# Reordering the softmax step of a fused attention and expert kernel: maxima first, the spread of the inverse sums between the exponentials

## The chip, the cores and the metric

One core of one Trainium2 chip runs the whole program. The metric is the time of one execution on the device in microseconds (us), as the median of several executions. The profiler records one execution; its span runs from its first to its last instruction.

## What is computed

The reference is one layer of cross attention and one feed-forward layer with a shared expert and eight routed experts, for 32 batches of 112 tokens with 512 channels, all in float32:

```python
x = x + attention(layernorm(x), ctx)      # 16 heads of 32 channels, causal
x = x + ffn(layernorm(x))                 # top 2 of 8 experts (352 wide) + a shared one (1408 wide)

# attention
scores = einsum('bhqd,bhkd->bhqk', qh, kh) / sqrt(32)
attn = softmax(where(causal, scores, min))
out = einsum('bhqk,bhkd->bhqd', attn, vh) @ Wout.T
```

The causal mask leaves only the first 112 of the 375 context rows for 112 queries, so the kernel works on 112 by 112 scores for each of the 16 heads of a batch. The softmax is computed as exp(score − maximum) without its division; the product with the values is divided by the row's sum afterwards.

## The kernel before

The program has three stages, one after the other: the attention with the norms and the router (stage A), the routed experts in 35 jobs of 256 tokens, and the shared expert with the final sum. The change touches stage A alone.

Stage A works on groups of four batches (g = 0 to 7, then two more rounds to drain what is under way). A group has a front and four steps (j = 0 to 3). The front transposes the normalised rows of the four batches, splits them into a high and a low part (`xT_hi` L811 on ScalarE, `xT_lo` L1133 on VectorE) and makes kT and qT, with 48 matmuls for qT alone. A step t = 4g + j works on several batches at once: the scores and exponentials of batch t, the transposed exponentials, value product and division of batch t−1, the output projection of batch t−2, and the second norm, its transposition and the router of batch t−3. A product of split operands is made of three matmuls on high and low parts, in the helper `product` (L542), so one line holds the q, k, value, projection and expert matmuls alike; they are told apart by their tiles.

The order of work on each engine is the order of the code; engines wait for each other by semaphores. There is no planner: the order is written by hand, separately in the program of each engine. In one step it is:

- TensorE: mask (L587) and scores (L596) into PSUM banks 0 to 3; transposes of the exponentials (`probsT`, L605); their products with the values of the batch (`outT`, L616); transposes of the spread inverse sums (`sumT`, L624), behind a wait for `rinv_spread`; the value product (into bank 4); the transposes of `xn2` (`normT`, L637); the projection (12 matmuls, `wout`, also into bank 4); the router (L660). At j = 2 of groups from 2 on, the rank matmuls (L667, L668) follow.
- ScalarE: four copies of `probsT` (L834); `rinv_wide` (L839), which spreads the 16 inverse sums of a row over 32 channels each; 8 exponentials (L849, each an ACTIVATE with an accumulator read); `rinvT` (L827), the copy of the transposed inverse sums; 8 exponentials; `aT_hi` (L860). At j = 3 two small exponentials of the router (L820, L821) come first.
- VectorE: `rinv` (L1142); the statistics of an input batch for the next group (L1093, L1096); `xn2` (L1099); at j = 0 the first choice of experts of the group before (`choose`, L1259 to L1274, ten chained small operations), at j = 3 the slots (`place`, L1294 to L1296, six operations); the maxima in two halves (`smax` L1159, `minus_max` L1161); `v_sb` (L1166), which empties bank 4; `xn2T` (L1174); `attnT` (L1181), the division; at j = 1 the second choice (L1277 to L1285); `xn` of the next group (L1099); `x` (L1196), which adds the projection; `logits` (L1201); at j = 2 the rank (L1207); statistics of `x1`; `aT_lo` (L1216). After step 2 the router's maxima (L1241 to L1243) follow.
- GpSimd: the inverse roots of the norms (L975, L977), at j = 3 the split of the next context (L984, L986), and eight indirect DMAs of token numbers (L1010) per group. The DMA queue of SP stores x1, the normalised rows and their transposes, and loads the next inputs.

The projection of a step takes bank 4 behind `v_sb`, which has to have emptied the value product from it:

```python
b = take(g, j, "proj")     # waits until bank 4 has been emptied as often as it was taken
product(bank(b, SEQ), [((aT_hi[...], aT_lo[...]), (wout_hi[...], wout_lo[...])) for k in range(KC)])
```

`TURNS` (L48 to L56) lists, for each bank from 4 to 7, which stage uses it after which; the counts of all `filled` and `emptied` waits come from it.

Of the kernel before, what the change touches and what calls it, by code (L numbers as in the profile page):

```python
# [14 lines left out]
P = 128  # L15
SEQ = 112
# [34 lines left out]
for _j in range(TB):  # L51
    TURNS += [((_j, "probsT", k), 1, (7, 5, 4, 6)[k]) for k in range(4)]
    TURNS += [((_j, "outT", 0), 1, 7), ((_j, "sumT", 0), 1, 5), ((_j, "value", 0), 0, 4),
              ((_j, "normT", 0), 3, 6), ((_j, "proj", 0), 2, 4), ((_j, "router", 0), 3, 6)]
    if _j == 2:
        TURNS += [((_j, "rank", 0), 2 * TB, 4)]  # L56
# [33 lines left out]
def build_program(nc, x, ctxT, wq, wkv, wout, gates, w_experts, w_shared, out):  # L90
# [17 lines left out]
    with ctx:  # L108
# [427 lines left out]
        def _(pe):  # L536
# [39 lines left out]
            def step(g, j):  # L576
# [42 lines left out]
                if there(g, j, 1):  # L619

                    pe.wait_ge(S["rinv_spread"], t)
                    b = take(g, j, "sumT")
                    for m in range(KC):
                        mm = pe.transpose(psum[:, b, m * SEQ:(m + 1) * SEQ], rinv_wide[:, 4 * m:4 * m + 4, :].rearrange("s h d -> s (h d)"),  # L624
                                          ident[0:SEQ, 0:SEQ])
                    mm.then_inc(filled[b], 1)
# [12 lines left out]

                def proj():  # L640
                    if there(g, j, 2):

                        if is_first(g):
                            pe.wait_ge(S["w_split"], 3)
                        pe.wait_ge(S["attnT_split"], t - 1)
                        b = take(g, j, "proj")
                        product(bank(b, SEQ), [((aT_hi[:, j % 2, k, :], aT_lo[:, j % 2, k, :]), (wout_hi[:, k, :], wout_lo[:, k, :]))
                                               for k in range(KC)]).then_inc(filled[b], 1)


                for part in ((proj, normT) if isinstance(g, int) and g >= NG else (normT, proj)):
                    part()
# [137 lines left out]
        def _(act):  # L790
# [7 lines left out]
            def body(g):  # L798
# [17 lines left out]
                for j in range(TB):  # L816
                    t = g * TB + j
                    if j == TB - 1 and there(g, 0, 4):
                        act.wait_ge(S["router_z"], 2 * g)
                        act.activation(rt["e"][:, :, :], rt["z"][:, :, :], ACT.Exp).then_inc(S["router_exp"], 1)  # L820
                        act.activation(rt1["ge"][:, :], rt1["g"][:, :], ACT.Exp, scale=-1.0).then_inc(S["router_exp"], 1)  # L821
                    def rinv_to_rows():
                        b = turns.bank("sumT")
                        if there(g, j, 2):
                            wait_emptied(act, g, j - 1, "outT")
                        wait_filled(act, g, j, "sumT")
                        act.activation(rinvT[:, :], bank(b, P, GT), ACT.Copy).then_inc(emptied[b], 1)  # L827

                    if there(g, j, 1):
# [6 lines left out]
                        if there(g, j, 2):  # L836
                            wait_filled(act, g, j - 1, "sumT")
                        act.wait_ge(S["rinv_made"], t)
                        act.activation(rinv_wide[:, :, :], rinv[:, :].unsqueeze(2).to_broadcast([SEQ, HEADS, HD]), ACT.Copy).then_inc(S["rinv_spread"], 1)  # L839
                        if not there(g, j, 0):  # L840
                            rinv_to_rows()
                    if there(g, j, 0):

                        at_least(act, S["rinv_made"], t - 1)
                        for i in range(2):
# [7 lines left out]
                            if i == 0 and there(g, j, 1):  # L853
                                rinv_to_rows()
                    if there(g, j, 1):

                        if there(g, j, 3):
                            wait_filled(act, g, j - 1, "proj")
# [220 lines left out]
        def _(dve):  # L1079
# [55 lines left out]
            def step(g, j):  # L1135
                t = g * TB + j
                if there(g, j, 1):
# [4 lines left out]
                    dve.reciprocal(rinv[:, :], rsum[:, (j + 1) % 2, :]).then_inc(S["rinv_made"], 1)  # L1142
                if before(g, NG - 1):
                    stats1(j, t + TB + 1, g + 2)
# [9 lines left out]
                if there(g, j, 0):  # L1154

                    dve.wait_ge(S["scores_done"], t + 1)
                    for i in range(2):
                        scores = psum[0:SEQ, 2 * i:2 * i + 2, 0:GT].rearrange("s r (m k) -> s r m k", m=4)
                        dve.tensor_reduce(smax[:, 2 * i:2 * i + 2, :], scores, AX.X, ALU.max).then_inc(S["smax_made"], 1)  # L1159
                        dve.wait_ge(S["smax_made"], 2 * t + i + 1)  # L1160
                        dve.tensor_scalar(minus_max[:, 2 * i:2 * i + 2, :], smax[:, 2 * i:2 * i + 2, :], -SCALE, None, ALU.mult).then_inc(S["max_made"], 1)  # L1161
                if there(g, j, 0):

# [11 lines left out]
                if there(g, j, 1):  # L1175

                    at_least(dve, S["attnT_split"], t - 1)
                    b = turns.bank("outT")
                    wait_emptied(dve, g, j, "sumT")
                    wait_filled(dve, g, j, "outT")  # L1180
                    dve.tensor_tensor(attnT[:, :], bank(b, P, GT), rinvT[:, :], ALU.mult).then_inc(emptied[b], 1)  # L1181
# [15 lines left out]
                if there(g, j, 3):  # L1197
# [3 lines left out]
                    dve.tensor_copy(logits[:, (j + 1) % TB, :], bank(b, SEQ, EXPERTS + 1)).then_inc(emptied[b], 1)  # L1201
                if j == 2 and routes(g):
# [294 lines left out]
```

## Time and profile before

| | |
|---|---|
| median of 3 executions | 1716.71 us (1716.38 to 1719.96) |
| profiled execution | 1713.32 us, span 1711.5 us |
| TensorE matmul busy | 1586.7 us (93% of the span) |
| VectorE busy | 883.5 us (52%) |
| ScalarE busy | 616.5 us (36%) |
| GpSimd busy | 463.2 us (27%) |
| mean granted TensorE clock | 0.972 of full speed |

The shares are means over the three stages. Stage A takes about the first 530 us; in it VectorE and ScalarE are busy half of the time or more, while they are mostly idle in the other two stages. Times in the trace are counted from the start of the span. A matmul's duration is modelled and overlaps the next one's, so the starts of matmuls tell more than their durations; the same holds for VectorE and ScalarE, where an instruction's record overlaps the next by about 0.1 us.

### The profile page before, as it was taken

What the parts mean: (1) busy time and instruction counts of PE and PEld (TensorE: products, weight loads), DVE (VectorE), ACT (ScalarE), POOL (GpSimd) and SP (SyncE); (2) the same over time, 40 slices, a digit from 0 to 9 for tenths busy, and PEclk for the clock granted to TensorE, in tenths of its full rate; (3) what the DMA queues carried; (4) which work ended last, traced back from release to release, by engine and by line L of the source; (5) the groups of instructions that cost most, each with busy time, mean ns of one, the idle gap of its engine ahead of it and who ended that gap; (6) DMA issues with size and microseconds to landing.
All of it is one profiled execution on the core that took longest, in us unless ns stands there. A gap on an engine that the chain in (4) does not pass through costs nothing.

```text
span 1711.5 us, 30372 instructions
## 1 busy us (share of the span) xinstructions
PE 1586.7 (93%) x10524; PEld 1329.2 (78%) x10524; DVE 883.5 (52%) x1724; ACT 616.5 (36%) x1945; POOL 463.2 (27%) x424
## 2 busy tenths in 40 slices
PE   4899899889993599999999999999999999999998
PEld 4677767767772499999999997888888888888886
DVE  4556675676565467676667675442232323232322
ACT  4766676576670232333332333321111111111111
POOL 3111312313213455655555550201000000000010
PEclk9899999999995699999999999999999999999999
DMA  5122322322122466666666664413020203021110
GB/s 186 52 61 86 87 83 59 86 80 75 43 87 44 152 236 238 259 243 240 240 232 249 244 254 161 140 70 111 13 99 25 98 25 98 25 86 36 50 49 25
DMA packets 82445, 202.43 MB, mean 118 GB/s; under 512 B 37424, under 2 KB 38448, under 8 KB 77648
## 3 DMA queue, kind: packets, MB, share of 16 engines
q1 hardware_dynamic: 70208, 168.44, 28.6%
q0 software_dynamic: 12176, 33.20, 5.9%
q8 instruction: 35, 0.57, 0.1%
q14 instruction: 26, 0.21, 0.1%
HBM read 153.64 MB, written 47.97 MB: 118 GB/s over the span
## 4 chain that ended last, share of the span: by engine, by line
PE 79%; DVE 8%; ACT 5%; issue 3%; DMA 1%; POOL 1%; another core or an unknown queue 1%; DVEq 0%; SPq 0%; ACTq 0%; POOLq 0%
PE psum L542 51%; PE psum L776 12%; PE psum L726 9%; ACT probs L849 2%; PE psum L699 2%; ACT probsT L834 2%; DVE smax L1159 2%; DVE stat L1093 1%; PE psum L596 1%; DVE v_sb L1166 1%; PE psum L587 1%; PE psum L605 1%; POOL lists_dram L1010 1%; PE psum L660 1%
## 5 line engine op out<-in xcount | busy, mean ns | idle before, releaser
L542 PE MATMUL psum<-nT_hi,ws_hi 128*128 128x512 f32 x616 | 243.1, 395 | 3.5 <-DVE nT_lo L1374 3.5
L542 PE MATMUL psum<-nT_hi,ws_lo 128*128 128x512 f32 x616 | 244.9, 398 | 0.0
L542 PE MATMUL psum<-nT_lo,ws_hi 128*128 128x512 f32 x616 | 244.4, 397 | 0.0
L1413 DVE TENSOR_TENSOR h_s<-psum,silu_s 128x512 f32<-128x512 f32 x77 | 53.2, 692 | 364.8 <-PE psum L542 360.5
L542 PE MATMUL psum<-gT_hi,wj_hi 128*128 128x256 f32 (+1 forms) x840 | 233.9, 278 | 1.2 <-DVE gT_lo L1345 1.2
L542 PE MATMUL psum<-gT_lo,wj_hi 128*128 128x256 f32 (+1 forms) x840 | 233.4, 278 | 0.0
L542 PE MATMUL psum<-gT_hi,wj_lo 128*128 128x256 f32 (+1 forms) x840 | 233.3, 278 | 0.0
L1072 POOL DMA_INDIRECT routed<-expert_out_dram,slot_b x56 | 55.2, 986 | 575.4 <-DVE slot_b L1426 383.2
L849 ACT ACTIVATE probs<-psum,minus_max 112x112 f32<-112x112 f32 x512 | 175.2, 412 | 16.5 <-DVE minus_max L1161 16.4
L1034 POOL TENSOR_SCALAR wj_hi<-wj_raw 128x2816 fp32r<-128x2816 f32 x68 | 136.8, 2028 | 145.1 <-PE psum L726 118.4
L1364 DVE TENSOR_TENSOR wj_lo<-wj_raw,wj_hi 128x2816 fp32r<-128x2816 f32 x70 | 170.3, 2434 | 5.7 <-issue 3.3
L542 PEld LDWEIGHTS psum<-gT_hi,wj_hi 128*128 128x128 f32 (+1 forms) x840 | 151.3, 180 | 8.0 <-issue 4.0
L542 PEld LDWEIGHTS psum<-gT_lo,wj_hi 128*128 128x128 f32 (+1 forms) x840 | 151.4, 180 | 2.4
L542 PEld LDWEIGHTS psum<-gT_hi,wj_lo 128*128 128x128 f32 (+1 forms) x840 | 151.4, 180 | 0.0
L939 ACT ACTIVATE silu_s<-psum 128x512 f32<-128x512 f32 x77 | 46.0, 598 | 286.4 <-PE psum L542 286.4
L1045 POOL DMA_INDIRECT xg<-normed_dram,job_ids x70 | 131.7, 1881 | 58.6 <-DMA job_ids<-lists_dram 44.6
L542 PEld LDWEIGHTS psum<-nT_hi,ws_hi 128*128 128x128 f32 x616 | 116.2, 189 | 31.9 <-issue 4.0
L542 PEld LDWEIGHTS psum<-nT_lo,ws_hi 128*128 128x128 f32 x616 | 115.9, 188 | 28.2
L542 PEld LDWEIGHTS psum<-nT_hi,ws_lo 128*128 128x128 f32 x616 | 116.1, 188 | 27.4
L849 ACT ACTIVATION_READ_ACCUMULATOR probs<-psum,minus_max 112x1 f32 x512 | 136.0, 266 | 0.0
L942 ACT ACTIVATE hs_hi<-h_s 128x512 fp32r<-128x512 f32 x77 | 48.7, 632 | 233.5 <-DVE h_s L1413 227.5
L776 PE MATMUL psum<-ws_lo,hs_hi 128*128 128x512 f32 x308 | 121.4, 394 | 0.0
(193 smaller groups left out, 3108.4 us busy)
## 6 DMA issues: line engine op xcount, KB each, us to landing
wj_raw<-in_w_experts SPq DMA_DIRECT2D x35, 2176.0 KB, 8.6
expert_out_dram<-y_c SPq DMA_DIRECT2D x35, 512.0 KB, 2.7
wj_raw<-in_w_shared SPq DMA_DIRECT2D x11, 768.0 KB, 4.4
x_in<-in_x SPq DMA_DIRECT2D x32, 224.0 KB, 3.5
x_res<-in_x SPq DMA_DIRECT2D x32, 224.0 KB, 3.0
x_dram<-x SPq DMA_DIRECT2D x32, 224.0 KB, 2.3
normed_dram<-xn SPq DMA_DIRECT2D x32, 224.0 KB, 3.1
normedT_dram<-xn2T SPq DMA_DIRECT2D x32, 224.0 KB, 3.5
```

What stands on the lines that cost most here:

```text
L542: mm = pe.matmul(out_ap, u, v, start=(n == 0), stop=(n == last))
L699: mm = pe.transpose(psum[:, b, j * P:(j + 1) * P], xg[p][:, j, k * P:(k + 1) * P], ident[:, :])
L726: mm = pe.matmul(bank(j), u, v, start=(i == 0 and q == 0), stop=(i == 2 and q == 2))
L776: mm = pe.matmul(bank(j), u, v, start=(i == 0 and q == 0), stop=(i == SC - 1 and q == 2))
L849: done = act.activation(probs[:, j % 2, 4 * r + m, :], psum[0:SEQ, r, m * SEQ:(m + 1) * SEQ], ACT.Exp, bias=minus_max[:, r, m:m + 1], scal ...
L939: act.activation(silu_s[:, :], bank(b), ACT.Silu).then_inc(emptied_b[b], 1)
L942: act.activation(hs_hi[:, i % 2, :], h_s[:, :], ACT.Copy).then_inc(S["hs_hi_made"], 1)
L1034: pool.tensor_scalar(wj_hi[p][:, part], wj_raws[p][:, part], 1.0, 0.0, ALU.mult, ALU.add).then_inc(S["wc_hi_made"], 1)
L1045: pool.indirect_dma_start(out=xg[p][:, j, :], out_offset=None, in_=normed_dram, in_offset=bass.IndirectOffsetOnAxis(ap=job_ids[p][:, j:j + ...
L1072: pool.indirect_dma_start(out=routed[:, b % 2, c, :], out_offset=None, in_=expert_out_dram, in_offset=bass.IndirectOffsetOnAxis(ap=slot_b[ ...
L1364: dve.tensor_tensor(wj_lo[p][:, cols], wj_raws[p][:, cols], wj_hi[p][:, cols].bitcast(F32), ALU.subtract).then_inc(S["wc_split"], 1)
L1413: dve.tensor_tensor(h_s[:, :], bank(b), silu_s[:, :], ALU.mult).then_inc(emptied_b[b], 1)
```

## The change

Three engines' programs are reordered; no operation is added or taken away.

1. VectorE: the maxima and their negated, scaled copies stand right behind `rinv`, ahead of the statistics, `xn2`, `choose` and `place`.
2. ScalarE: `rinv_wide` moves from ahead of the exponentials to between their two halves (where `rinvT` was), and `rinvT` moves behind the second half, ahead of `aT_hi`. Where a step has no exponentials (the drain), `rinv_wide` follows the `probsT` copies directly.
3. TensorE: the `sumT` transposes move from ahead of the value product to behind the `normT` transposes and ahead of the projection (in the drain: ahead of both). `TURNS` is reordered to match.
4. VectorE: `attnT`, which needs `rinvT`, moves from ahead of `xn` to behind `logits`.

```diff
--- before.py
+++ after.py
     TURNS += [((_j, "probsT", k), 1, (7, 5, 4, 6)[k]) for k in range(4)]
-    TURNS += [((_j, "outT", 0), 1, 7), ((_j, "sumT", 0), 1, 5), ((_j, "value", 0), 0, 4),
-              ((_j, "normT", 0), 3, 6), ((_j, "proj", 0), 2, 4), ((_j, "router", 0), 3, 6)]
+    TURNS += [((_j, "outT", 0), 1, 7), ((_j, "value", 0), 0, 4),
+              ((_j, "normT", 0), 3, 6), ((_j, "sumT", 0), 1, 5), ((_j, "proj", 0), 2, 4), ((_j, "router", 0), 3, 6)]
@@ TensorE
-                if there(g, j, 1):
-
-                    pe.wait_ge(S["rinv_spread"], t)
-                    b = take(g, j, "sumT")
-                    for m in range(KC):
-                        mm = pe.transpose(psum[:, b, m * SEQ:(m + 1) * SEQ], rinv_wide[:, 4 * m:4 * m + 4, :].rearrange("s h d -> s (h d)"),
-                                          ident[0:SEQ, 0:SEQ])
-                    mm.then_inc(filled[b], 1)
...
+                def sums():
+                    if there(g, j, 1):
+
+                        pe.wait_ge(S["rinv_spread"], t)
+                        b = take(g, j, "sumT")
+                        for m in range(KC):
+                            mm = pe.transpose(psum[:, b, m * SEQ:(m + 1) * SEQ], rinv_wide[:, 4 * m:4 * m + 4, :].rearrange("s h d -> s (h d)"),
+                                              ident[0:SEQ, 0:SEQ])
                         mm.then_inc(filled[b], 1)
...
-                for part in ((proj, normT) if isinstance(g, int) and g >= NG else (normT, proj)):
+                for part in ((sums, proj, normT) if isinstance(g, int) and g >= NG else (normT, sums, proj)):
                     part()
@@ ScalarE
+                    def rinv_across():
+                        if there(g, j, 2):
+                            wait_filled(act, g, j - 1, "sumT")
+                        act.wait_ge(S["rinv_made"], t)
+                        act.activation(rinv_wide[:, :, :], rinv[:, :].unsqueeze(2).to_broadcast([SEQ, HEADS, HD]), ACT.Copy).then_inc(S["rinv_spread"], 1)
+
...
-                        if there(g, j, 2):
-                            wait_filled(act, g, j - 1, "sumT")
-                        act.wait_ge(S["rinv_made"], t)
-                        act.activation(rinv_wide[:, :, :], rinv[:, :].unsqueeze(2).to_broadcast([SEQ, HEADS, HD]), ACT.Copy).then_inc(S["rinv_spread"], 1)
                         if not there(g, j, 0):
-                            rinv_to_rows()
+                            rinv_across()
...
                             if i == 0 and there(g, j, 1):
-                                rinv_to_rows()
+                                rinv_across()
                     if there(g, j, 1):
 
+                        rinv_to_rows()
                         if there(g, j, 3):
                             wait_filled(act, g, j - 1, "proj")
                         wait_emptied(act, g, j, "outT")
@@ VectorE
                     dve.reciprocal(rinv[:, :], rsum[:, (j + 1) % 2, :]).then_inc(S["rinv_made"], 1)
+                if there(g, j, 0):
+
+                    dve.wait_ge(S["scores_done"], t + 1)
+                    for i in range(2):
+                        ...
                 if before(g, NG - 1):
                     stats1(j, t + TB + 1, g + 2)
...
-                if there(g, j, 0):
-
-                    dve.wait_ge(S["scores_done"], t + 1)
-                    for i in range(2):
-                        ...
...
-                if there(g, j, 1):
-
-                    at_least(dve, S["attnT_split"], t - 1)
-                    b = turns.bank("outT")
-                    wait_emptied(dve, g, j, "sumT")
-                    wait_filled(dve, g, j, "outT")
-                    dve.tensor_tensor(attnT[:, :], bank(b, P, GT), rinvT[:, :], ALU.mult).then_inc(emptied[b], 1)
...
                     dve.tensor_copy(logits[:, (j + 1) % TB, :], bank(b, SEQ, EXPERTS + 1)).then_inc(emptied[b], 1)
+                if there(g, j, 1):
+
+                    at_least(dve, S["attnT_split"], t - 1)
+                    b = turns.bank("outT")
+                    wait_emptied(dve, g, j, "sumT")
+                    wait_filled(dve, g, j, "outT")
+                    dve.tensor_tensor(attnT[:, :], bank(b, P, GT), rinvT[:, :], ALU.mult).then_inc(emptied[b], 1)
```

## Rows read from the trace of the kernel before

**Rows 1.** Waits in 40 to 505 us: engine, line, releaser, us in total, times, longest.

```profile
PE psum L542 <- DVE v_sb L1166: 26.7, 30, 2.4
...
ACT probs L849 <- DVE minus_max L1161: 13.8, 12, 1.6
```

**Rows 2.** Timeline of step j = 1, group 4: start us, us, engine, line, instruction.

```profile
284.60 0.48 PE L542 MATMUL psum<-wout_hi,aT_hi 128*112 128x512 f32 x1 [0.40 <-DVE v_sb L1166]
...
287.67 0.69 DVE L1196 TENSOR_TENSOR x<-psum,x_res 112x512 f32<-112x512 f32 x1 [0.98 <-PE psum L542]
...
290.15 1.75 PE L605 MATMUL psum<-ident,probs 112*112 112x112 f32 x16
...
290.78 1.84 ACT L834 ACTIVATE probsT<-psum 112x448 f32<-112x448 f32 x4 [2.05 <-PE psum L605]
...
292.49 0.65 ACT L839 ACTIVATE rinv_wide<-rinv 112x512 f32<-112x512 f32 x1
...
293.01 0.38 ACT L849 ACTIVATE probs<-psum,minus_max 112x112 f32<-112x112 f32 x1
...
293.20 0.61 PE L624 MATMUL psum<-ident,rinv_wide 112*128 112x112 f32 x4
...
293.57 0.47 PE L542 MATMUL psum<-wkv_hi,ctx_hi 128*112 128x512 f32 x1
...
294.55 0.69 DVE L1166 COPY v_sb<-psum 112x512 f32<-112x512 f32 x1 [0.57 <-PE psum L542]
...
295.30 0.48 PE L542 MATMUL psum<-wout_hi,aT_hi 128*112 128x512 f32 x1 [0.40 <-DVE v_sb L1166]
...
295.64 0.62 ACT L827 ACTIVATE rinvT<-psum 128x448 f32<-128x448 f32 x1
...
296.29 0.62 DVE L1181 TENSOR_TENSOR attnT<-psum,rinvT 128x448 f32<-128x448 f32 x1 [0.52 <-ACT rinvT L827]
```

**Rows 3.** Timeline of step j = 2, group 4, the same columns.

```profile
302.12 0.64 DVE L1093 BATCH_NORM_STATS2 stat<-x_in 112x6 f32<-112x512 f32 x1
...
303.47 1.08 DVE L1159 TENSOR_REDUCE smax<-psum 112x8 f32<-112x896 f32 x1
...
305.89 0.69 DVE L1166 COPY v_sb<-psum 112x512 f32<-112x512 f32 x1
...
306.63 0.49 PE L542 MATMUL psum<-wout_hi,aT_hi 128*112 128x512 f32 x1 [1.06 <-DVE v_sb L1166]
```

**Rows 4.** Timeline of step j = 3, group 4, and the start of the next front.

```profile
311.17 0.19 DVE L1207 TENSOR_TENSOR rt_rank<-psum,list_at 112x32 f32<-112x32 f32 x1 [0.59 <-PE psum L668]
...
318.12 1.13 POOL L986 TENSOR_TENSOR ctx_lo<-ctx_in,ctx_hi 128x448 fp32r<-128x448 f32 x1
318.40 0.88 DVE L1161 TENSOR_SCALAR minus_max<-smax 112x8 f32<-112x8 f32 x1
...
319.92 0.48 PE L542 MATMUL psum<-wout_hi,aT_hi 128*112 128x512 f32 x1 [2.35 <-DVE v_sb L1166]
...
323.11 0.68 ACT L860 ACTIVATE aT_hi<-attnT 128x448 fp32r<-128x448 f32 x1
...
324.13 0.98 ACT L811 ACTIVATE xT_hi<-psum 128x448 fp32r<-128x448 f32 x2 [0.35 <-PE psum L559]
```

**Rows 5.** Timeline of front and step j = 0, group 4 (267 to 284 us), and the next projection.

```profile
270.34 0.19 DVE L1259 TENSOR_REDUCE rt_s<-rt_e 112x4 f32<-112x32 f32 x1 [1.23 <-DMA route_dram<-route]
...
272.48 0.19 DVE L1274 TENSOR_TENSOR rt_one<-prefer,route 112x32 f32<-112x32 f32 x1
...
279.68 1.09 DVE L1159 TENSOR_REDUCE smax<-psum 112x8 f32<-112x896 f32 x1 [7.00 <-PE psum L596]
...
345.66 0.48 PE L542 MATMUL psum<-wout_hi,aT_hi 128*112 128x512 f32 x1 [0.40 <-DVE v_sb L1166]
```

**Rows 6.** Busy times of two j = 3 projections: stretch, us, engines, PEclk, DMA.

```profile
257.60:262.00 4.40, 4.32 (x14) 3.24 (x15) 1.63 (x4) 3.93 (x21) 0.00 (x0) 0.66 0.00 0
319.90:323.00 3.10, 3.08 (x15) 2.39 (x16) 1.58 (x4) 3.10 (x18) 0.00 (x0) 1.00 0.00 0
```

More of the change, by code:

```diff
@@ L638, in normT @@
                         mm.then_inc(filled[b], 1)
+                def sums():
[5 more added lines that the diff above has]
+                                              ident[0:SEQ, 0:SEQ])
+                        mm.then_inc(filled[b], 1)
                 def proj():
@@ L1142, in step @@
                     dve.reciprocal(rinv[:, :], rsum[:, (j + 1) % 2, :]).then_inc(S["rinv_made"], 1)
+                if there(g, j, 0):
+                    dve.wait_ge(S["scores_done"], t + 1)
+                    for i in range(2):
+                        scores = psum[0:SEQ, 2 * i:2 * i + 2, 0:GT].rearrange("s r (m k) -> s r m k", m=4)
+                        dve.tensor_reduce(smax[:, 2 * i:2 * i + 2, :], scores, AX.X, ALU.max).then_inc(S["smax_made"], 1)
+                        dve.wait_ge(S["smax_made"], 2 * t + i + 1)
+                        dve.tensor_scalar(minus_max[:, 2 * i:2 * i + 2, :], smax[:, 2 * i:2 * i + 2, :], -SCALE, None, ALU.mult).then_inc(S["max_made"], 1)
                 if before(g, NG - 1):
@@ L1154, in step @@
                 if there(g, j, 0):
-                    dve.wait_ge(S["scores_done"], t + 1)
-                    for i in range(2):
[L1158 to L1161, printed above, removed]
-                if there(g, j, 0):
                     b = turns.bank("value")
```

## The prediction

> **What bounds the kernel now.** The change lies in stage A, so I read that stage alone. First the list of waits [rows 1]: TensorE waits 30 times for `v_sb` ahead of its projection, 26.7 us in all, and ScalarE only 12 times for the maxima, 13.8 us in all. Then the timelines. Each projection's first matmul is a milestone; I call it P and count a step from one P to the next. It is 295.30 − 284.60 = 10.70 us for j = 1 [rows 2], 11.33 for j = 2 [rows 2, 3], 13.29 for j = 3 [rows 3, 4] and 345.66 − 319.92 = 25.74 for j = 0, front included [rows 4, 5].
>
> Two chains compete for P. The reader can follow the first in [rows 2], in us behind P: the transposes start at 5.55, the ScalarE copies at 6.18, `rinv_wide` at 7.89, the `sumT` transposes at 8.60, the value product at 8.97, `v_sb` at 9.95, the next P at 10.70. This chain sets j = 1. The second is VectorE's own: `x` at 3.07, then its list of work up to `v_sb`, then P 0.74 us behind (305.89 to 306.63 [rows 3]). It sets j = 2 (with the second choice holding `x`) and j = 3, where TensorE is idle for 2.35 us [rows 4].
>
> **The change part by part.**
>
> *Maxima first.* The statistics and `xn2` cost 303.47 − 302.12 = 1.35 us ahead of the maxima [rows 3]. Moved behind, they let the exponentials start earlier: at j = 1 at 7.89, the slot of `rinv_wide`, instead of 8.41 [rows 2]. But VectorE does the same work ahead of `v_sb` as before, so its own chain isn't shortened.
>
> *`rinv_wide` between the halves.* Eight exponentials take 295.64 − 293.01 = 2.63 us, and the transposes follow `rinv_wide`'s start by 0.71 [rows 2]. So `sumT` can start at 7.89 + 2.63 + 0.71 = 11.23 behind P, not at 8.60. It stands right ahead of the projection, which it precedes by 0.37 (293.20 to 293.57): P at 11.60. The value product, now free of the sums, is done earlier, which gains nothing, for the projection is queued behind `sumT` on TensorE. Terms:
> - j = 1: 11.60 against 10.70, +0.90, seven times: +6.3.
> - j = 2: against 11.33, +0.27, five times (groups 2 to 6); groups 1 and 7 lack the second choice or the statistics, so I count them like j = 1, +0.9 each: together +3.2. The second choice now lies in the wait for the projection.
> - j = 3: with the router's exponentials and the rank some 0.7 more, 12.3, still under VectorE's 13.29: 0 in groups 2 to 6. Groups 0 and 1 have no slots to place and count like j = 1, +0.9 each; group 7 has no statistics, so that its VectorE chain is shorter: +0.3. Together +2.1.
> - steps 1 and 2 of the kernel have no earlier projection to count from; from the same chain +1.5.
>
> *Behind the scores at j = 0.* Before, VectorE stood idle for 7.00 us there, its statistics, `xn2` and `choose` being done [rows 5]. Now they are queued behind the wait for the scores and stand between maxima and `v_sb`: the maxima 2.42 us [rows 3], 1.35 [rows 3], ten choice operations 2.33 (270.34 to 272.48, and 0.19 [rows 5]), so `v_sb` starts 6.1 to 6.2 us behind `smax` and P 6.9, where the rows have 284.60 − 279.68 = 4.92 [rows 2, 5]. That is +2.0. By the first chain P would be at 5.8 (maxima not binding, exponentials from 2.1), so the choice binds. Five groups +10.0; group 1, without a choice, goes by the sums, +0.8; group 7, without statistics, +1.1: +11.9.
>
> *`attnT` behind `logits`.* Beside the projection it was free [rows 2]; now it is ahead of the `x1` statistics and `aT_lo`, about 0.55 us of VectorE. At j = 1 and 2 it is covered: VectorE reaches the maxima at 6.1 and still gives the first half by 7.4, ahead of 7.89, and `xn2` is done at 10.0, ahead of 11.23. At j = 3 it fills the 0.59 wait for the rank [rows 4]. Without that cover j = 3 would pay 0.55. Its later emptying of bank 7 (by 4.5) is ahead of the transposes at 5.55. At the end of a group it does cost: `attnT` would end at about 324.4 in these rows (`x` at 3.07 behind P, `logits`, 0.62), `aT_hi`, before at 323.11, follows and takes 0.68, and the front's `xT_hi`, before at 324.13, is queued behind it on ScalarE until 325.1 [rows 4]. Of this 0.95 later gaps may swallow some; bounds 0 and 0.95, and I take 0.65, nearer the row. Seven fronts: +4.6.
>
> *Queues.* `xn2` is 3 us later, and with it SP's store of it, its store of the transposes and the load of `x_in` behind them; each has a step or more until it is needed. GpSimd's inverse root of the moved statistics runs beside the choice. Its context split at j = 3 starts behind the value product, now about 1 us sooner relative to the maxima; before, one `minus_max` under `ctx_lo` took 0.88 us instead of 0.17 [rows 4]. Now `xn2` or `place` lie there. I take the same 0.7 and so no change; bounds −0.7 and +0.7 for six steps. The Trainium skill's GPSIMD Engine Reference, Key points, says that GpSimd shares its SBUF interfaces with VectorE and contends with instructions that have two SBUF inputs, which `place` is made of; by that rule the time could grow by up to 4 us more.
>
> *Clock.* Of the five j = 3 projections in groups 2 to 6 three (groups 2, 3 and 6; one stands there) ran at a mean granted clock near 0.66, so in good part at the 1.2 GHz level, and took 4.4 us instead of 3.1 [rows 6], behind TensorE's idle 2.35 us. The change puts 2 to 3 us of idle or near-idle TensorE ahead of P at j = 0 too. No row shows what shorter, broken idle does. Bounds: nothing lost, or 1.3 at each of some 28 steps (+36); I take half of six, +4.
>
> Sum: 6.3 + 3.2 + 2.1 + 1.5 + 11.9 + 4.6 + 4 = 33.6 us. On the profiled execution's 1713.3 us that is 1746.9. The median of the runs shown lies 3.4 above that execution, so 1750.3. The two later stages are untouched.
>
> **The rivals.**
>
> *Clock lost at most steps.* Every step gets a broken wait of about 2 us ahead of its projection. For it: [rows 6]. Against it: j = 3 waits longer than that and kept its clock in two groups of five, of which one is in [rows 6]. Time: 1716.7 + 29.6 + 36 = 1782. The Trainium skill's page TensorE: Matmul & The Clock Gate, Part 1, has the slow clock as the default that only activity releases; by that rule this rival is as likely as the rows leave it. Chance 0.12.
>
> *The choice and the front hide.* If the j = 0 projection doesn't wait for the choice and the front doesn't lose to `aT_hi`, the sums alone decide (+0.8 at each j = 0): 1716.7 + 6.3 + 3.2 + 2.1 + 1.5 + 5.6 = 1735. Against it: bank 4 ties the projection to `v_sb`. Chance 0.15.
>
> *Faster.* The value product no longer waits for the sums: `v_sb` could start 0.7 us earlier at some 31 steps, and if the projection followed it, −22 us: 1695. It decides only if `rinv_wide` reaches TensorE by 9.9 behind P. It would need the first half of the exponentials in 1.3 us, against 2.63 in the rows. Chance 0.04.
>
> *No effect.* The gains at the maxima (of ScalarE's waits for them, 13.8 us [rows 1]) and the losses cancel, if what I call chains have slack: 1717. Chance 0.03.
>
> **How the numbers follow.** My forecast has 0.66 and a range of its own of 1738 to 1766 (front 0 to 0.95, sharing ±4, clock 0 to +16). A measurement can tell about 0.2%, 3.4 us, from no change. Only the two last rivals aren't slower: faster 0.04, same 0.03, slower 0.93. The range for 8 in 10 takes in most of the hidden-choice rival and part of the clock one: 1733 to 1775.
>
> **What would show it.** In the changed profile: `sumT` transposes about 11.2 us behind P at j = 1, waiting for `rinv_wide`, with P 0.4 behind; steps of 11.6 for j = 1 and 2 and about 13.3 for j = 3; at j = 0 the choice between maxima and `v_sb`, with a TensorE wait of over 2 us for `v_sb`; no ScalarE wait left for `minus_max` at j = 1 to 3; ahead of the front `aT_hi` some 1.4 us later behind P. Wrong would be: steps of 10.7 or less with the sums filled in time, or projections at the slow level at j = 1 and 2.

## The result and the profile after

| | before | changed |
|---|---|---|
| median of the first measurement | 1717.97 us | 1751.37 us (4 executions, 1746.24 to 1756.70) |
| ratio, 95% interval | | 1.0190 (1.0157 to 1.0223) |
| measured again later | 1718.47 us | 1750.02 us, 1.0175 (1.0152 to 1.0199) |
| profiled execution | 1713.32, span 1711.5 us | 1755.53, span 1753.8 us |
| mean granted clock | 0.972 | 0.966 |

The change costs 33.4 us, in the repetition 31.5 us; 33.6 was forecast. The page of the changed kernel's profile, its head and its first part:

```profile
span 1753.8 us, 30368 instructions
PE 1601.8 (91%) x10524; PEld 1333.3 (76%) x10524; DVE 882.7 (50%) x1724; ACT 616.9 (35%) x1945; POOL 466.6 (27%) x424
```

The same number of matmuls is busy for 15 us more than before, all of it in stage A. The records of the projections have 8.8 of these 15 us, and a projection's record is longer at the lower clock (0.74 us for 0.47 in the rows of group 5 below). So TensorE's loss isn't all new waiting. For the remaining 6 us it isn't shown that they are clock, since records that stand apart also overlap less. The work of the other engines is what it was.

The waits of stage A in the changed kernel (40 to 545 us; the columns are those of [rows 1]):

```profile
DVE smax L1153 <- PE psum L596: 98.8, 10, 13.4
ACT aT_hi L865 <- DVE attnT L1206: 75.6, 30, 5.5
...
PEld psum L638 <- ACT rinv_wide L828: 34.1, 31, 2.4
PE psum L638 <- ACT rinv_wide L828: 27.0, 31, 1.9
...
PE psum L629 <- DVE xn L1104: 15.2, 24, 1.2
...
PE psum L542 <- DVE v_sb L1171: 4.4, 9, 0.9
...
ACT probs L853 <- DVE minus_max L1155: 2.6, 1, 2.6
```

Against [rows 1]: TensorE's wait for `v_sb` has gone from 26.7 to 4.4 us, ScalarE's for the maxima from 13.8 to 2.6 (one wait, at 41.9 us, that the kernel before has too), and both were what one would like to see go. In their place TensorE waits 31 times for `rinv_wide`, 27.0 us, and 24 times for `xn2` (L1104), 15.2 us. A list of waits alone doesn't tell that the kernel became slower; the steps do.

Step j = 1 of group 3 in the changed kernel's timeline, P at 238.26, to be held against [rows 2]:

```profile
238.26 0.47 PE L542 MATMUL psum<-wout_hi,aT_hi 128*112 128x512 f32 x1
...
241.31 0.69 DVE L1194 TENSOR_TENSOR x<-psum,x_res 112x512 f32<-112x512 f32 x1 [2.61 <-PE psum L542]
242.19 0.62 DVE L1206 TENSOR_TENSOR attnT<-psum,rinvT 128x448 f32<-128x448 f32 x1
...
244.34 1.03 DVE L1153 TENSOR_REDUCE smax<-psum 112x8 f32<-112x896 f32 x1
...
246.14 0.38 ACT L853 ACTIVATE probs<-psum,minus_max 112x112 f32<-112x112 f32 x1
...
248.19 0.68 DVE L1171 COPY v_sb<-psum 112x512 f32<-112x512 f32 x1
...
248.78 0.70 ACT L828 ACTIVATE rinv_wide<-rinv 112x512 f32<-112x512 f32 x1
...
249.53 0.60 PE L638 MATMUL psum<-ident,rinv_wide 112*128 112x112 f32 x4 [0.59 <-ACT rinv_wide L828]
249.90 0.47 PE L542 MATMUL psum<-wout_hi,aT_hi 128*112 128x512 f32 x1
```

The exponentials start 7.88 us behind P (246.14 − 238.26), `rinv_wide` 10.52, the `sumT` transposes 11.27, the next P 11.64. `v_sb` starts at 9.93, so bank 4 is free in time; the projection stands behind `sumT` in TensorE's queue and follows that.

Step j = 0 of group 5 in the same timeline, from the first maxima to P, against [rows 5]:

```profile
363.56 1.09 DVE L1153 TENSOR_REDUCE smax<-psum 112x8 f32<-112x896 f32 x1 [11.94 <-PE psum L596]
...
366.06 0.69 DVE L1098 BATCH_NORM_STATS2 stat<-x_in 112x6 f32<-112x512 f32 x1
...
367.61 0.18 DVE L1264 TENSOR_REDUCE rt_s<-rt_e 112x4 f32<-112x32 f32 x1
...
367.75 0.60 PE L629 MATMUL psum<-ident,xn 112*128 112x112 f32 x4 [0.50 <-DVE xn L1104]
...
369.17 0.60 PE L638 MATMUL psum<-ident,rinv_wide 112*128 112x112 f32 x4 [0.82 <-ACT rinv_wide L828]
...
369.57 0.19 DVE L1279 TENSOR_TENSOR rt_one<-prefer,route 112x32 f32<-112x32 f32 x1
...
369.91 0.69 DVE L1171 COPY v_sb<-psum 112x512 f32<-112x512 f32 x1
370.66 0.74 PE L542 MATMUL psum<-wout_hi,aT_hi 128*112 128x512 f32 x1 [0.89 <-DVE v_sb L1171]
```

VectorE is idle for 11.94 us ahead of the scores, where it was 7.00, and does statistics, `xn2` and the choice behind them, so `v_sb` starts 6.35 and P 7.10 us behind `smax`. TensorE's wait ahead of P comes in three pieces, 0.50, 0.82 and 0.89 us. This projection ran at the slow level: its matmul record has 0.74 us in place of 0.47.

The steps of stage A, P to P, by j, from the timelines, in us. The first four columns are the sum of the seven steps of groups 1 to 7; the last is the median of groups 2 to 6:

| kernel | j = 0 | j = 1 | j = 2 | j = 3 | medians of j = 0, 1, 2, 3 |
|---|---|---|---|---|---|
| before | 183.1 | 75.1 | 78.1 | 89.3 | 25.74, 10.70, 11.33, 13.29 |
| changed | 198.7 | 87.3 | 82.9 | 88.9 | 29.13, 13.20, 11.65, 12.83 |
| changed, repeated | 199.8 | 83.1 | 82.2 | 92.9 | 29.47, 11.67, 11.66, 12.82 |
| changed with filler work | 196.0 | 81.6 | 81.5 | 88.6 | 27.92, 11.67, 11.64, 12.83 |

The last kernel, an experiment below (its second profile), has all projections of these steps at the full clock. A slow projection can be told by its twelve matmuls, whose starts then spread over 3.7 us or more instead of 2.6. Up to t = 30 the profile of before has three, all at j = 3, and each of the two of the changed kernel has seven; the last projections, in the drain, are slow in every kernel.

The profiled execution shown above is one of the longer ones: at its last projection (t = 33) it is 38.4 us later than before, in the repetition 35.5. Of the 38.4 the table has 32.2, the first two projections 4.0 (repetition 2.0), the drain 2.2 (1.1). Behind the last projection come 1190 us before and 1194 (1193) changed. This part spreads from 1190 to 1198 us over the profiles of all kernels, and no edit touches it. One step of the changed kernel stands out: at t = 12 ScalarE starts its `probsT` copies 2.63 us behind the transposes (3.48 in the repetition), in every other kernel 0.63 to 0.68. P stands 7.98 (9.83) us behind `smax` there, and 7.33 in the first experiment, which has the same order on VectorE. The cause of this pause is open.

### The profile page after: what moved, and what is told of

Its sections match the earlier page's. It is cut to its first block, busy times and chain, and to the rows that moved or that the text cites. A ratio compares the mean times of both kernels' runs of the same rounds, so it can differ in the third digit from the quotient of the medians.

```text
span 1753.8 us, 30368 instructions
## 1 busy us (share of the span) xinstructions
PE 1601.8 (91%) x10524; PEld 1333.3 (76%) x10524; DVE 882.7 (50%) x1724; ACT 616.9 (35%) x1945; POOL 466.6 (27%) x424
## 4 chain that ended last, share of the span: by engine, by line
PE 78%; ACT 7%; DVE 7%; issue 3%; DMA 2%; POOL 1%; another core or an unknown queue 1%; SPq 0%; DVEq 0%; ACTq 0%; POOLq 0%
PE psum L542 50%; PE psum L778 12%; PE psum L728 8%; ACT probs L853 4%; ACT probsT L842 2%; PE psum L701 2%; PE psum L596 1%; PE psum L587 1%; DVE smax L1153 1%; DVE stat L1098 1%; PE psum L662 1%; DMA wj_raw<-in_wout 1%; POOL lists_dram L1015 1%; PE psum L638 1%; PE psum L605 1%
## 5 line engine op out<-in xcount | busy, mean ns | idle before, releaser
L853 ACT ACTIVATION_READ_ACCUMULATOR probs<-psum,minus_max 112x1 f32 x512 | 142.6, 279 | 0.0
L542 PEld LDWEIGHTS psum<-nT_hi,ws_lo 128*128 128x128 f32 x616 | 116.1, 189 | 27.4
L980 POOL TENSOR_SCALAR rs<-mv 112x1 f32<-112x1 f32 x64 | 22.3, 348 | 399.0 <-DVE mv L1101 257.8
```

The lines of the kernel that those rows point to most:

```text
L542: mm = pe.matmul(out_ap, u, v, start=(n == 0), stop=(n == last))
L853: done = act.activation(probs[:, j % 2, 4 * r + m, :], psum[0:SEQ, r, m * SEQ:(m + 1) * SEQ], ACT.Exp, bias=minus_max[:, r, m:m + 1], scal ...
```

## The experiments

Each result is the median difference to the kernel before as measured in the same session, with the ratio and its 95% interval.

**Maxima first, alone.** The kernel before with this one move on VectorE:

```
  rinv
+ maxima (smax, minus_max, two halves)
  stats1, xn2, choose / place
- maxima
```

> The kernel before with VectorE's maxima moved behind rinv and nothing else. Theory A (two chains per step, from one projection start P to the next): steps j = 1 and 2 stay at 10.7 and 11.3 us since the inverse sums are still spread ahead of the exponentials; j = 3 falls by 0.45 to about 12.8; at j = 0 of groups 2 to 6 P comes 7.0 us behind the first smax instead of 4.9, as the choice is queued between them: +9 us in all, +4 more if the clock falls there, so a median of 1726 to 1731. Theory B (VectorE's new order slows every step because v_sb comes later): j = 1 at 11.6 and above 1740.

+12.0 us, 1.0073 (1.0045 to 1.0102). The part that is meant to bring exponentials forward costs on its own. At j = 0 its seven steps take 191.6 us against 183.1, since choice and statistics now stand behind the wait for the scores; at j = 1 and 2 the medians are what they were (10.71, 11.35), and j = 3 gains 0.45 a step. Two j = 0 projections (t = 8 and 12) ran slow, and the j = 1 steps behind them took 12.28 and 13.44 us, so the sum of j = 1 is 4.2 us longer.

**The old order at j = 0 alone.**

```
- maxima first
+ maxima first if j != 0, behind choose if j == 0
```

> The changed kernel, but at j = 0 VectorE keeps the old order (statistics, xn2, choice, then the maxima). Theory A: smax to P at j = 0 falls from 7.1 to about 5.8 us (then the sums bind: 2.1 to the first exponential, 2.63 for eight, 0.71, 0.37), steps j = 1 and 2 stay at 11.65: -1.3 at six steps, and with it part of the slow projections behind that wait: 1735 to 1745. Theory B (the choice is hidden behind the sums anyway): 1751, no change from the changed kernel.

+24.1 us, 1.0137 (1.0120 to 1.0154), so the order at j = 0 carries some 9 us of the 33. The kernel's timeline, j = 0 of group 5:

```profile
356.40 1.09 DVE L1152 TENSOR_REDUCE smax<-psum 112x8 f32<-112x896 f32 x1 [6.04 <-PE psum L596]
...
361.94 0.60 PE L638 MATMUL psum<-ident,rinv_wide 112*128 112x112 f32 x4 [1.53 <-ACT rinv_wide L828]
362.31 0.47 PE L542 MATMUL psum<-wout_hi,aT_hi 128*112 128x512 f32 x1
```

P is 5.91 us behind `smax`, against 7.10 with the choice there and 4.92 before: of the 2.18 the choice has 1.19 beyond what the late sums alone take, 0.99. Without one cause the other is still there.

**`rinv_wide` ahead of both halves.** The changed kernel with one call moved on ScalarE; `rinvT` stays behind the second half:

```
  probsT copies
+ rinv_across()
  first half of the exponentials
- rinv_across()
  second half, rinvT
```

> The changed kernel, but ScalarE spreads the inverse sums (rinv_wide) ahead of the exponentials, as before; rinvT, attnT and the order on TensorE stay as changed. Theory A: the transposes of the sums don't wait any more, steps j = 1 fall from 11.65 to about 10.9 (bound by xn2, its transposes and the sums' own 0.37) and j = 2 to 11.0 to 11.3; j = 0 and j = 3 stay (28.2 and 12.8): about -9, so 1738 to 1745. Theory B (VectorE's chain with attnT in it is what made 11.65): steps stay at 11.6 and the time at 1751.

+13.2 us, 1.0081 (1.0064 to 1.0098). The right cause, mis-sized: 1727.47 us, below the expected range of 1738 to 1745. In its two measurements the changed kernel cost 33.4 and 31.5 us, so 18 to 20 hang on this one place. The timeline of j = 1, group 5, P at 350.60:

```profile
350.60 0.49 PE L542 MATMUL psum<-wout_hi,aT_hi 128*112 128x512 f32 x1 [1.93 <-DVE v_sb L1168]
...
358.50 0.65 ACT L828 ACTIVATE rinv_wide<-rinv 112x512 f32<-112x512 f32 x1
...
360.69 0.60 PE L629 MATMUL psum<-ident,xn 112*128 112x112 f32 x4 [0.72 <-DVE xn L1101]
361.13 0.55 PE L638 MATMUL psum<-ident,rinv_wide 112*128 112x112 f32 x4
361.45 0.47 PE L542 MATMUL psum<-wout_hi,aT_hi 128*112 128x512 f32 x1
```

Its step is 10.85 us. Three of the five j = 1 steps of groups 2 to 6 are 12.4 us long in this profile, each behind a slow projection at j = 0, so the place of `rinv_wide` takes away four of the seven slow projections and not all. The sums, ready early, stand behind the transposes of `xn2`, which have no wait left to hide in once the maxima go ahead of `xn2`: a second, smaller end of the step, that the order on TensorE makes.

**Filler matmuls.** The changed kernel with matmuls that serve only to keep TensorE at work (`ident` by `mask`, into the bank that `sumT` then overwrites), run twice under two names:

```
- (normT, sums, proj)
+ (filler(2), normT, filler((9, 2, 2, 4)[j]), sums, proj)
```

> The changed kernel with filler matmuls (112 rows by 448 columns, into the bank that the sums overwrite) in TensorE's waits ahead of the projection: 2 before the transposes of xn2, and 9, 2, 2, 4 behind them at j = 0, 1, 2, 3. They are extra work whose results are overwritten. Theory A (what the chains leave unexplained, about 10 us, is TensorE's clock falling in the broken waits): no projection at the slow level outside the start, steps behind j = 0 fall from 13.2 to 11.7, and the time falls by about 10 us to 1738 to 1745. Theory B (clock unaffected by how the waits are filled): 1751 or a little more.

> The kernel of e4 once more beside the changed kernel. Theory A (clock): 8 to 12 us less than the changed kernel in the same call, 1737 to 1742. Theory B (the difference seen before was between chips): equal to it.

+24.6 us, 1.0138 (1.0121 to 1.0155), and +23.1 us, 1.0126 (1.0108 to 1.0145). In the second session the changed kernel itself had +31.5 (below): 8.4 us less time by more work, and no execution of the one overlaps the other's (1746.9 to 1754.7 against 1739.5 to 1743.3). The busy times of single projections show how. First the changed kernel, at t = 16 and 17 (columns: stretch, us, then PE, PEld, DVE, ACT, POOL busy, granted clock, DMA share, GB/s):

```profile
303.80:309.40 5.60, 5.51 (x15) 4.08 (x15) 1.03 (x4) 1.68 (x9) 0.00 (x0) 0.51 0.00 0
318.00:321.10 3.10, 3.10 (x19) 2.40 (x17) 2.33 (x13) 2.71 (x15) 0.00 (x0) 1.00 0.00 0
```

and the kernel with filler, from its second profile, at t = 16 and 20:

```profile
300.40:303.50 3.10, 3.10 (x15) 2.40 (x16) 0.95 (x3) 1.57 (x9) 0.00 (x0) 1.00 0.00 0
364.40:367.50 3.10, 3.09 (x15) 2.40 (x16) 0.95 (x3) 1.60 (x9) 0.00 (x0) 1.00 0.00 0
```

The projection of t = 16 takes 5.5 us at a granted 0.51, that is almost wholly at the 1.2 GHz level, and 3.1 at 1.00, 2.4 GHz. The loss isn't made good later: the step behind it is 14.12 us instead of 11.64. At j = 1, 2 and 3 the fillers themselves hold nothing up: the median steps with them and those of the repeated changed kernel agree within 0.02. At j = 0 the nine do where no choice covers them, at t = 4 and 28: P is 6.55 and 6.49 us behind `smax` there, 5.97 without filler. So the clock is worth some 1 us more than the 8.4. The kernel before was not run with filler.

**`attnT` back.** The kernel of the third experiment with `attnT` and `rinvT` in their old places:

```
+ attnT ahead of choose(g - 1, 1) and xn
- attnT behind logits
+ rinvT between the halves
```

> The kernel of e3 (sums spread ahead of the exponentials) with rinvT back between the two halves and attnT back ahead of xn, as before; the maxima stay first and TensorE's order stays as changed. Theory A (attnT ahead of the statistics of x1 costs 0.55 us of VectorE's chain where nothing covers it, and 0.3 to 0.65 at each front, but shortens the wait of the second choice at j = 1): j = 1 at 10.4 (from 10.85), j = 2 at 11.3 to 11.5 (from 10.86), smax at j = 0 at 20.2 to 20.3 behind P instead of 20.8: about -3 against e3, so 1722 to 1727. Theory B (attnT's place is worth more than these, since it holds aT_hi and the front): 1715 or less.

+8.7 us, 1.0055 (1.0039 to 1.0072). That is 4.5 us less than with both moved, but in another session and with intervals that overlap, so the times alone don't show it. The timelines do: at the end of a group the next `smax` stands 20.14 us behind P instead of 20.77, 0.63 at each front where neither kernel is disturbed. The step j = 2 pays for part of it, 11.69 us in place of 10.87.

**The slots behind the projection's start.** This tries the reading of VectorE's chain in [rows 3, 4]: the kernel before, where `place` only moves into VectorE's wait for the projection.

```
- place(g - 1) ahead of the maxima, j == 3
+ place(g - 1) behind xn, ahead of x, j == 3
```

> The kernel before, and only VectorE's six slot operations at j = 3 moved from ahead of the maxima to behind xn, where VectorE waits for the projection. Theory A (v_sb at the end of VectorE's chain sets j = 3): the step falls from 13.29 by 1.4 to about 11.9 in groups 2 to 6, -7 us, and TensorE's wait there shrinks, so that fewer projections run at the slow level, up to -4 more: 1703 to 1709. Theory B (the step is set by the maxima and the exponentials, or x is delayed instead): no change, 1714.

−13.4 us, 0.9928 (0.9907 to 0.9948). The steps j = 3 fall from 13.29 to 11.34 in the median, by 1.95 where 1.4 was expected, and no projection up to t = 30 ran slow. The six operations have the 1.4. The other 0.55 is that the second `minus_max` no longer lies beside GpSimd's split of the context: it takes 0.17 us, where it took 0.88 [rows 4].

**All that helps.** The maxima first only at j = 1 to 3, `rinv_wide` ahead of both halves, `sumT` ahead of `normT` on TensorE, `attnT` late only at j = 1, and the slots late:

```
+ maxima first if j != 0, in the old place if j == 0
+ rinv_across() ahead of both halves, rinvT between them
+ (sums, normT, proj)
+ attnT behind logits if j == 1, else in its old place
+ place(g - 1) behind xn
```

> A candidate from the findings. Maxima first only at j = 1 to 3 (at j = 0 the old order), rinv_wide ahead of the exponentials and rinvT between their halves as before, the sums transposed behind the value product and ahead of the transposes of xn2, attnT behind logits only at j = 1 and as before elsewhere (at j = 1 the second choice of experts stands ahead of x), and the slots at j = 3 behind xn. Theory A: steps of 10.4, 10.7 and 11.4 for j = 1, 2, 3 in groups 2 to 6 and 25.1 for j = 0, together -20 us against the kernel before, less some clock: 1690 to 1700. Theory B (the engines' work per step, not the chains, is the floor; TensorE's own work in a step is about 9.8 us): gains only at j = 3, about 1705.

−21.9 us, 0.9877 (0.9856 to 0.9897), 1694.75 us (1694.20 to 1696.85): faster than both kernels. Its page and its timeline at j = 3:

```profile
span 1693.1 us, 30372 instructions
PE 1586.0 (94%) x10524; PEld 1324.2 (78%) x10524; DVE 881.9 (52%) x1724; ACT 616.2 (36%) x1945; POOL 463.2 (27%) x424
```

```profile
305.11 0.68 DVE L1172 COPY v_sb<-psum 112x512 f32<-112x512 f32 x1
...
305.85 0.49 PE L542 MATMUL psum<-wout_hi,aT_hi 128*112 128x512 f32 x1
...
308.03 0.18 DVE L1305 TENSOR_TENSOR rt_eq<-rt_rank,rt_one 112x32 f32<-112x32 f32 x1
...
309.13 0.17 DVE L1307 CAST slots_i<-route 112x4 int32<-112x4 f32 x1
...
309.64 0.69 DVE L1205 TENSOR_TENSOR x<-psum,x_res 112x512 f32<-112x512 f32 x1 [0.34 <-DVE slots_i L1307]
```

The slots end 3.45 us behind P (309.13 + 0.17 − 305.85) and hold `x` back by 0.7 us, to 3.79 behind P instead of 3.08; no step is longer for it. The median steps are 25.27, 10.63, 10.86 and 11.18 us. So the first idea of the change, maxima ahead of VectorE's list, is part of a faster kernel, though not at j = 0. What it gives there by itself was not measured; the slots alone have 13.4 of the 21.9 us.

**The maxima back behind the slots.** The changed kernel without its first part:

```
  rinv
- maxima
  stats1, xn2, choose / place
+ maxima
```

> The changed kernel, but the maxima back in their old place behind xn2, choice and slots. Theory A (with the sums behind the first eight exponentials, the maxima's place sets the step): first exponential at j = 1 and 2 at about 8.7 behind P instead of 7.9, steps of 12.4 instead of 11.65; j = 3 at 14.2 instead of 12.8; smax to P at j = 0 5.9 instead of 7.1: +11 us against the changed kernel, so 1755 to 1765. Theory B (the maxima's place does not matter, only the sums'): steps of 11.65, and 1740 to 1750.

+77.0 us, 1.0449 (1.0427 to 1.0470), that is 1793.64 us: missed, for the expected range ended at 1765. Up to t = 29 its profile has 21 slow projections. Two of them, t = 17 and 19:

```profile
332.90:337.50 4.60, 4.60 (x18) 3.38 (x16) 1.34 (x8) 2.67 (x15) 0.00 (x0) 0.63 0.00 0
363.40:368.20 4.80, 4.80 (x16) 3.54 (x16) 0.00 (x0) 2.43 (x13) 0.00 (x0) 0.59 0.00 0
```

**The same with filler.** To see whether the surplus is the clock:

```
- (normT, sums, proj)
+ (normT, filler((5, 7, 7, 13)[j]), sums, proj)
```

> The kernel of e8 (maxima in the old place) with filler matmuls ahead of the sums: 5, 7, 7, 13 at j = 0 to 3. Theory A (e8's surplus over the 11 us that its chains give is the clock: its projections ran at the slow level at most steps): steps of about 12.5 for j = 1 and 2 and 14.4 for j = 3, projections of 3.1 to x at all of them, and 30 us or more less than e8: 1755 to 1765. Theory B (e8's longer steps come from a dependency that the chains leave out): still above 1780.

+42.9 us, 1.0238 (1.0214 to 1.0262), so some 34 us of the 77 are the clock's (the two were measured in two sessions). Two projections of this kernel, t = 17 and 19:

```profile
320.50:323.60 3.10, 3.10 (x18) 2.41 (x17) 1.40 (x8) 2.74 (x15) 0.00 (x0) 1.00 0.00 0
347.60:350.70 3.10, 3.10 (x18) 2.41 (x17) 0.00 (x1) 2.75 (x15) 0.00 (x0) 1.00 0.00 0
```

Its median steps at j = 1 to 3 are 12.57, 12.48 and 14.63 us, by 0.9, 0.8 and 1.8 more than with the maxima first. With the sums between the halves a delay of the maxima reaches P, less some slack: at t = 21 `smax` starts 1.4 us later than with the maxima first and P comes 0.9 later, at t = 23 it is 2.8 and 1.8.

**The changed kernel again**, beside the fillers.

> The changed kernel once more, beside the fillers on one chip. Expected 1745 to 1755 by all theories; it gives the number that the two fillers are compared with, and how much it scatters: by the clock theory more than they do (where a projection meets the slow level differs from run to run).

+31.5 us, 1.0175 (1.0152 to 1.0199). Its profile has slow projections at other steps than the first (t = 2, 6, 7, 8, 10, 14 and 23, against 7, 8, 15, 16, 20, 23 and 25): where they fall changes from execution to execution; their number is the same in these two.

**Filler at j = 0 alone.**

```
- (normT, sums, proj)
+ (normT, filler((9, 0, 0, 0)[j]), sums, proj)
```

> The changed kernel with filler matmuls only at j = 0 (9, ahead of the sums). Theory A (the long wait for v_sb behind the choice is where the clock falls, and the projection behind it runs slow): most of e10's gain, 1738 to 1744. Theory C (the short waits of j = 1 to 3 add up to the same): slow projections remain at j = 1 to 3 and the time lies halfway, near 1745.

+23.8 us, 1.0132 (1.0113 to 1.0152): nearly all that filler at every step gives, 23.1. No filled projection is slow in this profile, but three others are: t = 9 and 21, one step behind filled ones, and t = 7, at j = 3. So the time fell as the first theory had it, and slow projections remain as the other had it. Why slow projections at j = 3 became fewer too (one, against three and two in the profiles of the changed kernel) is open.

## Why the prediction was right, point by point

**The chain of the sums (j = 1, j = 2).** Right. `sumT` 11.27 us behind P (11.23 worked out), P 0.37 behind it, steps of 11.64 and 11.65 (11.60). The projection follows the sums and not `v_sb`. The third experiment, which undoes this alone, shows it as the dearest part: 18 to 20 us with the clock it loses.

**Behind the scores at j = 0.** Right: `smax` to P 7.10 us for the 6.9 of the sum, a term of 2.18 in place of 2.0. TensorE waits for over 2 us, as foretold, but not for `v_sb` alone: 0.50 us for `xn2`, 0.82 for the sums and 0.89 for `v_sb`, together 2.21. Over all seven groups `smax` to P takes 13.8 us more than before, for the 11.9 forecast; some 0.7 of that is ScalarE's pause at t = 12.

**j = 3.** The forecast was no change; the step fell to 12.83. The step of the prediction that failed is "I take the same 0.7" for the sharing of GpSimd and VectorE. In the changed kernel's timeline, j = 3 of group 4, the context split meets another instruction:

```profile
338.54 0.17 DVE L1155 TENSOR_SCALAR minus_max<-smax 112x8 f32<-112x8 f32 x1
...
340.91 0.57 POOL L989 TENSOR_SCALAR ctx_hi<-ctx_in 128x448 fp32r<-128x448 f32 x1
341.16 0.34 DVE L1301 CAST slots_i<-route 112x4 int32<-112x4 f32 x1
341.56 1.14 POOL L991 TENSOR_TENSOR ctx_lo<-ctx_in,ctx_hi 128x448 fp32r<-128x448 f32 x1
341.74 0.69 DVE L1171 COPY v_sb<-psum 112x512 f32<-112x512 f32 x1 [0.23 <-DVE slots_i L1301]
342.49 0.49 PE L542 MATMUL psum<-wout_hi,aT_hi 128*112 128x512 f32 x1 [0.31 <-DVE v_sb L1171]
```

`minus_max` takes 0.17 us where it took 0.88 [rows 4], and the last small operation of the slots 0.34 for 0.17: 0.2 lost in place of 0.7, −0.46 for the step, inside the bound of −0.7. It is so in all of groups 2 to 6 (0.34 to 0.35 us; before, `minus_max` took 0.88 to 0.97). `v_sb` still sets P there.

Both of the stretched instructions have one input in SBUF. The prediction says of `place` that it is made of instructions with two; two of its six are (`rt_eq`), and neither lay beside the split. So these steps don't test what it took from the Trainium skill's GPSIMD Engine Reference, Key points, and the 4 us didn't come. That page names VectorE's 2-port mode as well as two SBUF inputs; no record here tells an instruction's mode. At the start of the kernel before, two-input operations do meet the split, and there it is GpSimd's instruction that is long, 4.26 us where it otherwise takes 0.56 (at the start of the changed kernel `ctx_lo` takes 3.15 for 1.13). No experiment was made on it:

```profile
13.20 4.26 POOL L984 TENSOR_SCALAR ctx_hi<-ctx_in 128x448 fp32r<-128x448 f32 x1
...
14.75 2.28 DVE L1114 TENSOR_TENSOR wq_lo<-wj_raw,wq_hi 128x2048 fp32r<-128x2048 f32 x1
```

**The front.** The mechanism was right, the term of 4.6 was too large. Between P and the start of qT lie 9.03 us in place of 8.41, +0.62 for the 0.65 taken; `aT_hi` starts 1.5 us later behind P (4.67 for 3.18; 1.4 was foretold), and putting `attnT` back returns 0.63 a front. But the trace of before loses some 0.4 to 0.7 us between that start and the maxima that the later kernels mostly don't: at t = 20 in its qT stream, at t = 24 behind it. So `smax` is 20.81 and 20.58 us behind the last P before, and 20.76 and 20.83 in the kernel with filler; at t = 4 and 8 the front does show, 20.62 and 20.44 against 21.14 and 20.94. Over the seven fronts P to `smax` takes 1.8 us more in the changed kernel, each of the two profiles having three of them behind a slow projection. Where the loss in the kernel before comes from is open.

**Clock.** The size taken, +4, was right as a net, and its parts were larger, which is luck: half of six was a guess between two bounds. The changed kernel loses 8.4 us to slow projections (repetition against filler), and the kernel before already loses some 4.3 in its three (behind them qT starts 10.03, 9.75 and 9.82 us behind P, at t = 20 and 24 it is 8.41 and 8.42). The slow projections came at j = 0 and 3 above all, but also at j = 1 and 2, which the prediction had named as what would be wrong. Those behind which a j = 1 step begins cost that step 1.6 us, and 2.5 at t = 16, in place of the 1.3 taken: that projection ran almost wholly at the slow level, and its matmul starts spread over 4.83 us in place of 2.63.

The broken waits go with the slow projections. With the maxima back and no filler TensorE is idle for 2.4 to 3.9 us in each step at j = 1 to 3 of group 3, and most projections are slow; in the changed kernel for 1.3 to 1.6, and seven are; with filler for 0.5, and none of these steps is. In the kernel before it is idle for 0.4, 1.05 and 2.35 us at j = 1, 2 and 3, and its three slow projections are all at j = 3.

**The sum.** Without any clock loss the forecast was 29.6. Measured: 23.1 us with filler against the kernel before (interval 18.6 to 24.9), and 4.3 that the kernel before has in its own slow projections, 27.4. The 2.2 between them are no more than the noise. That 33.6 met 33.4 is luck in part, for the terms missed in both directions. The 28 steps of the table grew by 32.2 us; the forecast had 32.1 for them:

| term | forecast | two profiles |
|---|---|---|
| j = 1 and 2, without their slow projections | 9.5 | 10.0 |
| behind the scores at j = 0 | 11.9 | 13.8 |
| front | 4.6 | 1.8 |
| j = 3 | 2.1 | −0.4 |
| clock (steps j = 1 and 2 behind a slow projection) | 4 | 7.0 |

Outside the table the forecast had 1.5 for the first steps (4.0, repetition 2.0) and nothing for the drain (2.2 and 1.1).

**The rivals.** That the clock is lost at most steps didn't come about (1782): seven projections of some thirty. The rule of the Trainium skill named there, page TensorE: Matmul & The Clock Gate, Part 1, has activity release the slow clock, and the fillers agree: with them the granted clock of the projections shown is 1.00. The kernel with the maxima back, whose steps j = 1 to 3 are 0.8 to 1.8 us longer by waiting, did lose the full clock at most steps. So that rival is true of a kernel one move away from this one. That choice and front hide (1735) is refuted for the choice by the old order at j = 0, 9 us faster; the front delays qT by 0.62 us, but little of it reached the time, so in that half the rival was nearer than the forecast. The faster one needed `rinv_wide` by 9.9 us behind P; it came at 10.52. That condition wasn't the only one: in the third experiment it came at 7.90, and the step was still 10.85, for `v_sb` hadn't moved to 0.7 us earlier. It stood 9.93 us behind P in the changed kernel and 9.95 before, held by VectorE's own list. The rival did hold a truth: with the sums early and the slots moved, the steps do fall below those of before.

## What to carry to other kernels

Before an operation is moved up on one engine, look at what is queued behind it and then at the chain that ends the step: here the maxima were given the front place on an engine that wasn't late for them, while the sums, on which the end of each step hangs, were put behind eight exponentials. Small chained work that nobody awaits soon belongs into a wait that stays in any case: the six slot operations, moved behind the start of the projection, gave 13.4 us by themselves. And a wait ahead of a long TensorE product can be paid twice, once as a wait and once in the clock of the product, even when it is broken into pieces; here the pieces ahead of a slow projection of the changed kernel were 0.3 to 1.03 us long, 1.3 to 2.2 in all. Filler matmuls tell the two apart.

## What was not expected of the hardware

- More work made the kernel faster: 8.4 us in the changed kernel, some 34 us in the one with late maxima, by matmuls whose result is thrown away.
- The granted clock made delays compound: moving the maxima back adds 19.8 us when the clock is held (42.9 against 23.1) and some 45 when it isn't (77.0 against 31.5, in two sessions).
- Filler in front of a quarter of the projections did nearly the whole of what filler in front of all did (23.8 against 23.1 us).
- Beside GpSimd's split of the context one small VectorE instruction took 0.88 us instead of 0.17 in one order and another 0.34 instead of 0.17 in the next; at t = 7 of the changed kernel a 112x512 `xn` took 1.50 instead of 0.54. The `v_sb` copy, which reads PSUM, had its usual 0.69 under the same split.
